# A four-block convolution kernel on one core: a new order of its units, a written-out TensorE program and a new head

## What is computed

```
x = x + attention(gn(x))      # block 0: windows of 4 x 4 pixels, 16 heads of size 1, softmax over 16 keys,
                              #          relative position bias, then a 16 x 16 projection
x = x + conv3x3(gn(x))        # block 1 ("conv1")
x = x + grid(gn(x))           # block 2: 16 cells, 4 columns x 4 rows; each a 3 x 3 convolution of up to 48
                              #          channels to "right", "up" and "down", with bias and relu;
                              #          the last cell's "right" is the output
x = x + quantised_conv(gn(x)) # block 3: x scaled by the largest value over all 8 images, rounded, 3 x 3
```

## Time and profile before

| | us |
|---|---|
| median of three runs | 3185.96 |
| lowest and highest | 3176.93, 3187.13 |
| the profiled execution | 3186.43 |
| its span, first to last instruction | 3184.6 |
| TensorE busy in the span | 2787.8 (88%) |
| VectorE busy | 2328.2 (73%) |
| ScalarE busy | 2012.8 (63%) |

### The profile page before, as it was taken

How to read it: one execution, slowest core, us unless ns; L and a number is a source line. 1 busy time by engine, 2 the same in 40 slices (tenths; PEclk the granted TensorE clock), 3 DMA queues, 4 the chain that set the end, 5 groups by cost and what they waited for, 6 DMA issues and landing times.

```text
span 3184.6 us, 86914 instructions
## 1 busy us (share of the span) xinstructions
PE 2787.8 (88%) x39155; PEld 1177.1 (37%) x39155; DVE 2328.2 (73%) x2062; ACT 2012.8 (63%) x2317; POOL 23.3 (1%) x68
## 2 busy tenths in 40 slices
PE   3564799989999899989999899989998998989976
PEld 2552233333333333333333333333333343333323
DVE  7978995889878895889688995899698971240135
ACT  1103976677767676767767676766766775766624
POOL 0000000000000000000000000000000000000000
PEclk9886899999999999999999999999999999999998
DMA  2003566577756866477756766587657755685667
GB/s 62 7 4 51 77 78 90 75 93 103 88 89 82 113 73 98 62 98 99 89 81 88 107 74 94 72 112 84 82 83 95 100 77 77 85 111 72 79 87 180
DMA packets 66136, 268.42 MB, mean 84 GB/s; under 512 B 48848, under 2 KB 49488, under 8 KB 53328
## 3 DMA queue, kind: packets, MB, share of 16 engines
q1 hardware_dynamic: 65744, 262.57, 60.2%
HBM read 22.54 MB, written 12.04 MB: 11 GB/s over the span
## 4 chain that ended last, share of the span: by engine, by line
PE 68%; DVE 13%; ACT 9%; issue 7%; SPq 1%; DMA 1%; POOLq 0%; POOL 0%; DVEq 0%; ACTq 0%
PE conv_banks L827 43%; PE conv_banks L841 19%; ACT pair L680 4%; ACT half L680 3%; DVE half L1030 2%; PE side_banks L788 2%; DVE score_max L1119 1%; DVE pair L1030 1%; PE stat_bank L798 1%; ACT scores L666 1%; PE side_banks L754 1%; PE conv_banks L926 1%; DVE pair L1116 1%; PE conv_banks L862 1%; DVE scores L1045 1%
## 5 line engine op out<-in xcount | busy, mean ns | idle before, releaser
L827 PE MATMUL conv_banks<-pair,w_cells 128*32 128x392 f32 x17664 | 1542.9, 498 | 48.2 <-issue 30.3
L680 ACT ACTIVATE pair<-conv_banks,b_cells 32x784 f32<-32x784 f32 x1316 | 1214.0, 923 | 568.4 <-PE conv_banks L841 502.4
L841 PE MATMUL conv_banks<-half,w_cells 64*32 64x392 f32 x18432 | 879.7, 509 | 140.0 <-ACT pair L680 60.1
L827 PEld LDWEIGHTS conv_banks<-pair,w_cells 128*32 128x32 f32 x17664 | 550.7, 109 | 983.3 <-issue 925.1
L680 ACT ACTIVATE half<-conv_banks,b_cells 32x392 f32<-32x392 f32 (+1 forms) x780 | 520.9, 668 | 199.9 <-PE conv_banks L841 128.0
L841 PEld LDWEIGHTS conv_banks<-half,w_cells 64*32 64x32 f32 x18432 | 339.5, 108 | 661.2 <-issue 611.6
L1030 DVE TENSOR_SCALAR half<-conv_banks,b_cells 32x392 f32<-32x392 f32 (+1 forms) x180 | 114.4, 636 | 327.1 <-PE conv_banks L841 168.8
L1030 DVE TENSOR_SCALAR pair<-conv_banks,b_cells 32x784 f32<-32x784 f32 x220 | 227.5, 1034 | 111.8 <-PE conv_banks L841 101.7
L1043 DVE TENSOR_TENSOR scores<-qkv 128x1792 f32<-128x1792 f32 x98 | 197.9, 2020 | 94.9 <-ACT qkv L661 94.7
L666 ACT ACTIVATE scores<-scores 128x1792 f32<-128x1792 f32 x104 | 176.7, 1699 | 101.1 <-DVE scores L1121 57.5
L1053 DVE TENSOR_REDUCE score_max<-scores 128x112 f32<-128x1792 f32 x98 | 197.9, 2020 | 9.5
(11 more groups left out here) (100 smaller groups left out, 1093.9 us busy)
## 6 DMA issues: line engine op xcount, KB each, us to landing
pair<-pair SPq DMA_DIRECT2D x384, 391.9 KB, 8.6
half<-half SPq DMA_DIRECT2D x352, 192.4 KB, 5.4
x_block<-in_x SPq DMA_DIRECT2D x64, 98.0 KB, 5.3
stream<-in_xs SPq DMA_DIRECT2D x8, 784.0 KB, 9.1
x_scratch<-stream SPq DMA_DIRECT2D x7, 784.0 KB, 7.7
pair<-x_scratch SPq DMA_DIRECT2D x7, 784.0 KB, 14.2
out_dram<-pair SPq DMA_DIRECT2D x4, 1120.0 KB, 5.4
half<-half SPq DMA_DIRECT2D x176, 7.1 KB, 4.6
```

Source lines behind the costliest of these rows:

```text
L680: done = nc.scalar.activation(dst, src, ACT.Relu, bias=b_ap)
L827: done = nc.tensor.matmul(conv_ps[32 * q:32 * q + 32, n + b, 0:QN], w, P[row][:, QG * s + BG * (q // 2):QG * s + BG * (q // 2 + 1), BX * ( ...
L841: done = nc.tensor.matmul(conv_ps[32 * q:32 * q + 32, n + h, 0:QN], w_all[rows, at:at + 32], T[rows, QG * u + BG * (q // 2):QG * u + BG * ...
```

## The change

- The list of units is one text (`ORDER`, a star marks the units of the later columns, which belong to the earlier image). It mixes units of different cells, where the list before went cell by cell; which cell a unit opens is found by `starts`.
- VectorE's share of the emptying is named unit by unit and by stop: `("s", j)` is behind scores j, `("w", j)` behind weigh j. In a middle round it has 18 units (before: the 20 of column 0), in round 6 43 (before 20), in round 7 10 (before 16), in round -1 one (before none). `finish` and the move of the stream have other stops.
- The side steps of TensorE, ScalarE and SP stand at other places, in all rounds.
- TensorE's loop over rounds 0 to 4 is written out; the other engines keep theirs.
- The head: x is laid out on the host so that it comes in one transfer; TensorE's first steps and VectorE's statistics wait only for what they read; ScalarE runs one small exponential at the start; the position bias is also laid out transposed (`first_rel`); the maximum over 16 keys is four `max` operations on halves; the last sums come in another order; the first stream is normed ahead of the next image's statistics; and the halos of the first image's normed input are issued half by SP and half by ScalarE.

The core of the diff (of the tables those of a middle round, and round -1's and the others' only in part):

```diff
-BODY = [((3, 0), 1), ((2, 2), 1), ((3, 1), 1), ((2, 3), 1), ((0, 0), 0), ((3, 2), 1), ((0, 1), 0), ((3, 3), 1),
-        ((0, 2), 0), ((1, 0), 0), ((0, 3), 0), ((1, 1), 0), ((1, 2), 0), ((2, 0), 0), ((1, 3), 0), ((2, 1), 0)]
-EARLY_BODY = [x for x in BODY if not x[1]]
-LATE_BODY = [x for x in BODY if x[1]]
...
+ORDER = """
+30D0* 30D1* 22D0* 22U0* 22D1* 22U1* 22R0* 00R0 22R1* 23U0* 23U1* 31D0* 31D1* 23R0* 23R1* 00D0 00D1
+00R1 32D0* 32D1* 01D0 01U0 01U1 01R0 01D1 33R0* 33R1* 10D0 10D1 01R1 02U0 02R0 02U1 02R1 02D0 10R0
+02D1 10R1 11U0 11D0 11U1 03U0 03U1 11D1 11R0 11R1 12U0 12U1 03R0 12D0 03R1 20D0 12D1 20D1 12R0 20R0
+20R1 12R1 21D0 21U0 21U1 21D1 21R0 13U0 13U1 13R0 13R1 21R1
+"""
+def unit(text):
+    return (int(text[0]), int(text[1])), "RUD".index(text[2]), int(text[3])
+def units(text):
+    return [unit(t) for t in text.split()]
+UNITS = units(ORDER)
+UNITS_F = [unit(t) for t in ORDER.split() if t[4:] != "*"]
+UNITS_L = [unit(t) for t in ORDER.split() if t[4:] == "*"]
...
-PE_MID = {2: [("qkv", 1, 0)], 7: [("proj", 0, 0), ("qkv", 2, 0)], 12: [("proj", 1, 0), ("qkv", 3, 0)],
-          27: [("proj", 2, 0), ("qkv", 4, 0)], 44: [("proj", 3, 0), ("qkv", 5, 0)],
-          49: [("proj", 4, 0), ("qkv", 6, 0)], 54: [("proj", 5, 0)], 59: [("proj", 6, 0)], 60: [("mean1", 0, 0)],
-          61: [("var1", 0, 0), ("mean0", 0, 1)], 62: [("var0", 0, 1)], 64: [("qkv", 0, 1)],
-          65: [("conv1", 0, 1)], 66: [("conv1", 1, 1)], 67: [("mean2", 0, 1), ("var2", 0, 1)]}
...
+            5: [("proj", 0, 0)], 8: [("qkv", 2, 0)], 13: [("proj", 1, 0), ("qkv", 3, 0)],
+            19: [("proj", 2, 0), ("qkv", 4, 0)], 25: [("proj", 3, 0), ("qkv", 5, 0)],
+            32: [("proj", 4, 0), ("qkv", 6, 0)], 41: [("proj", 5, 0)], 42: [("proj", 6, 0)],
+            43: [("mean1", 0, 0), ("var1", 0, 0), ("mean0", 0, 1), ("var0", 0, 1)], 45: [("qkv", 0, 1)],
+            46: [("conv1", 0, 1)], 47: [("conv1", 1, 1)], 49: [("mean2", 0, 1), ("var2", 0, 1)]}
+PE_MID = {1: [("qkv", 1, 0)], 8: [("proj", 0, 0), ("qkv", 2, 0)], 14: [("proj", 1, 0)], 17: [("qkv", 3, 0)],
+          29: [("proj", 2, 0)], 30: [("qkv", 4, 0)], 42: [("proj", 3, 0)], 43: [("qkv", 5, 0)],
+          48: [("proj", 4, 0)], 51: [("qkv", 6, 0)], 57: [("proj", 5, 0)], 60: [("proj", 6, 0)],
+          61: [("mean1", 0, 0), ("var1", 0, 0), ("mean0", 0, 1), ("var0", 0, 1)], 63: [("qkv", 0, 1)],
+          64: [("conv1", 0, 1)], 65: [("conv1", 1, 1)], 66: [("mean2", 0, 1)], 67: [("var2", 0, 1)]}
...
+ACT_MID = {1: [("qkv", 1, 0), ("exp", 1, 0)], 7: [("exp", 2, 0)], 8: [("qkv", 2, 0)], 10: [("exp", 3, 0)],
+           11: [("exp", 4, 0)], 17: [("qkv", 3, 0)], 19: [("exp", 5, 0)], 25: [("exp", 6, 0)],
+           34: [("qkv", 4, 0)], 37: [("exp", 7, 0)], 43: [("exp", 8, 0), ("qkv", 5, 0)], 45: [("exp", 9, 0)],
+           48: [("exp", 10, 0)], 51: [("qkv", 6, 0), ("exp", 11, 0)], 56: [("exp", 12, 0)],
+           57: [("exp", 13, 0)], 62: [("qkv", 0, 1)], 67: [("exp", 0, 1)]}
...
+SP_FIRST = {0: [("xb", 1)], 1: [("input", 0)], 29: [("xa", 2)], 42: [("conv1", 1)], 43: [("xb", 2)],
             49: [("input", 1)]}
-SP_MID = {35: [("x3", -1)], 48: [("xa", 2)], 63: [("conv1", 1)], 66: [("xb", 2)], 67: [("input", 1)]}
-SP_BEFORE = {35: [("x3", -1)], 62: [("conv1", 1)], 67: [("input", 1)]}
-SP_LATE = {35: [("x3", -1)]}
+SP_MID = {52: [("x3", -1), ("xa", 2)], 54: [("conv1", 1)], 67: [("xb", 2), ("input", 1)]}
...
-SHARED_FIRST, SHARED_MID, SHARED_LATE, SHARED_LAST = [], [(0, 0), (0, 1), (0, 2), (0, 3)], [(0, 0), (0, 1), (0, 2), (0, 3)], [(3, 0), (2, 2), (3, 1), (2, 3), (3, 2)]
...
+VEC_FIRST = {("w", 0): "00D1"}
+VEC_MID = {("w", 0): "22D0",
+           ("s", 5): "23R0 23R1 00D0 00D1",
+           ("s", 6): "01D0 01U0 01U1 01R0 01D1",
+           ("s", 7): "01R1 02U0 02R0 02U1 02R1 02D0 10R0 02D1"}
+FINISH_AT = ("s", 11)
+MOVE_AT_FIRST, MOVE_AT = ("s", 9), ("w", 13)
+VEC_LATE = """22U0 22U1 22R0 31D1 23R0 23R1 00D0 00D1 00R1 32D0 32D1 01D0 01U0 01U1 01R0 01D1 10D1 01R1 02U0 02R0
+02U1 02R1 02D0 10R0 02D1 11U1 03U0 03U1 11R0 12U0 12U1 03R0 12D0 03R1 20D0 12D1 20R0 12R1 21U0 21U1
+13U0 13U1 13R0"""
+VEC_LAST = """22U0 22R1 23U0 23U1 31D0 31D1 23R0 23R1 32D0 32D1"""
+SHARED_FIRST, SHARED_MID = [[u for text in at.values() for u in units(text)] for at in (VEC_FIRST, VEC_MID)]
+SHARED_LATE, SHARED_LAST = units(VEC_LATE), units(VEC_LAST)
...
+                sp.dma_start(XA[:], xa[i]).then_inc(x_in, 16)
...
+                if isinstance(i, int) and i == 0:
+                    send_side(sp, INPUT, 0)
+                    send_seam(sp, INPUT, 0)
+                else:
+                    send_half(sp, INPUT)
...
+            def first_halo(which):
+                act.wait_ge(c_ready, (which + 1) * NQ)
+                send_side(act, INPUT, 64)
+                send_seam(act, INPUT, 1)
...
+            act.wait_ge(half_set, 1)
+            nc.scalar.activation(warm[:], minus_half[:], ACT.Exp).then_inc(warmed, 1)
...
-            with pe.Fori(0, B - 3) as m:
+            for m in range(B):
                 body(m)
-            body(B - 3)
-            body(B - 2)
...
-                if k >= 1:
+                if 1 <= k < WROWS - 1:
                     first_num(k - 1)
...
+            first_num(WROWS - 2)
+            first_num(WROWS - 1)
             side_step(-2, "proj", WROWS - 2)
-            first_num(WROWS - 1)
             side_step(-2, "proj", WROWS - 1)
...
-                    rel = relb[:].rearrange("p (a b) -> p b a", b=WPX).unsqueeze(2).to_broadcast(shape)
+                    rel = first_rel.rearrange("p (b a) -> p b a", b=WPX).unsqueeze(2).to_broadcast(shape)
                     e4 = e.rearrange("p b (w a) -> p b w a", a=WPX)
                     first.inc(nc.vector.tensor_tensor(e4, q, key, ALU.mult))
                     first.wait()
                     first.inc(nc.vector.tensor_tensor(e4, e4, rel, ALU.add))
                     first.wait()
+                    first.inc(nc.vector.tensor_tensor(first_max, e[:, 0:8], e[:, 8:16], ALU.max))
+                    first.wait()
+                    for n in (4, 2):
+                        first.inc(nc.vector.tensor_tensor(first_max[:, 0:n], first_max[:, 0:n], first_max[:, n:2 * n],
+                                                          ALU.max))
+                        first.wait()
                     dve.wait_ge(scores_ready, j)
-                    first.inc(nc.vector.tensor_reduce(mx[:], e.rearrange("p b n -> p n b"), AX.X, ALU.max))
+                    first.inc(nc.vector.tensor_tensor(mx[:], first_max[:, 0], first_max[:, 1], ALU.max))
                     first.wait()
...
+                first_divide(WROWS - 1)
                 residual(0, WROWS - 2)
-                first_divide(WROWS - 1)
-                turn(0, first, None, True)
+                xb = XB[:].rearrange("p g w -> p (g w)")
+                dve.wait_ge(x1_ready, WROWS - 1)
+                for c in range(NQ - 1):
+                    first.inc(nc.vector.bn_stats(st1[:, c, :], xb[:, c * QN:(c + 1) * QN]))
+                residual(0, WROWS - 1)
+                dve.wait_ge(x1_ready, WROWS)
+                first.inc(nc.vector.bn_stats(st1[:, NQ - 1, :], xb[:, (NQ - 1) * QN:]))
+                first.hold()
+                nc.vector.bn_aggr(mv1[:], st1[:].rearrange("p c k -> p (c k)")
+                                  ).then_inc(norm_sems[1]["meanvar_ready"], 1)
+                norm(0, 1, first, mv1, dev1[:], nm1)
+                normalise_stream(1, nm1, 0)
+                dve.wait_ge(x_in, 2 * 16)
+                block_stats(0, XA[:], st0, mv0, first)
+                norm(1, 0, first, mv0, nm0[:, 3:4], nm0)
+                normalise_chunk(1, 0)
...
+            def other_work(m, at):
+                early = isinstance(m, int) and m < 0
+                empty(m, units((VEC_FIRST if early else VEC_MID).get(at, "")))
+                if at == FINISH_AT and not early:
+                    finish(m, m)
+                if at == (MOVE_AT_FIRST if early else MOVE_AT):
+                    move_stream(m + 1)
...
```

More of the change, by code:

```diff
@@ L153, in count_halos @@
             wrote(m, "input", INPUT)
-        for (cell, late) in body_of(m):
-            need[m, cell] = [(key, n[key]) for key in in_places(*cell)]
-            for o in cell_outs(*cell) if cell != LAST else []:
+        for k, (cell, o, u) in enumerate(units_in(m)):
+            if starts(m, k):
+                need[m, cell] = [(key, n[key]) for key in in_places(*cell)]
+            if u == 1 and cell != LAST:
                 wrote(m, (cell, o), out_place(*cell, o))
-        if m == -1:
-            n_first = dict(n)
     return need
@@ L179 @@
 PE_FIRST = {0: [("qkv", 0, 0), ("conv1", 0, 0), ("conv1", 1, 0), ("mean2", 0, 0), ("var2", 0, 0), ("qkv", 1, 0)],
[L180 to L184, removed]
@@ L191 @@
[L191 to L197, removed]
-             13: [("exp", 5, 0)], 16: [("exp", 6, 0)], 19: [("qkv", 4, 0), ("exp", 7, 0)], 23: [("exp", 8, 0)],
```

(44 more changed lines are left out.)

135 lines of the change are left out of this document (73 added, 62 removed).

## The result

The changed kernel takes 3141.2 us (median of 4 runs, 3134.7 to 3144.0) against 3186.6 for the kernel before in the same session: a ratio of 0.986, 95% interval 0.984 to 0.989. It is faster, but by 45 us where 172 were forecast, and 3141 lies above the range of 2980 to 3095. Its profiled execution (3140.0 us, 3138.3 in the span) is the one read here.

A forecast was written before the change was run, and what follows sets the result against it. TensorE was taken as the bound from 289.6 us on, VectorE's attention before. Round -1 ending at 523, + 5 x 333 + 331 + 310 + 115 + 68.1 of tail + 1.8 gave 3014 us; range 2980 to 3050, to 3095 with rival 1.

The forecast's parts named there:

- Head: Everything before the first unit: 41 us less (4 to 48), with the first unit's matmuls at 248 us.
- Scores and table load: In the head: faster bias addition and maximum save 26 us together; moving the table load ahead saves 1.3.
- The start: Start of the head: x in one transfer and earlier statistics, beginning near 9.8 us, gain 4 (3 to 5.5).
- The part between the last residual and the first unit: End of head: norming the stream first and sharing halo issuing between SP and ScalarE gain 3 us (2 to 5).
- Round -1: Round before round 0: moving ScalarE work to VectorE and four small units among large ones saves 8.5 us (0 to 15).
- TensorE's loop: Round edges: writing out the loop removes four jumps, 34 to 39 us; 14 if only the first gap were the jump's.
- New order and shares: Middle rounds: TensorE's 324.3 us floor plus 8.4 of waits, 333 a round (325 to 342).
- signs of being wrong: Rounds staying at 342 us, VectorE without a gap in them, or ScalarE standing at the edge.
- Rival 1: Rounds: the order gives nothing, VectorE comes late and each round keeps its 17 us: 3089 us; chance 0.26.
- Rival 2: Round edges: stalls move to ScalarE's loop, its jump costing 8 us; 24 us more, 3038; chance 0.10.
- Rival 3: Round edges: the stall isn't the loop's, written-out code changes nothing and 34 us stay: 3048; chance 0.05.
- Rival 4: SP's queue: 20R and 21U stand behind SP's wait, costing 29 us in each of six rounds: 3188; chance 0.03.

The follow-up runs named there:

- b_pe: The kernel before with only TensorE's loop over the rounds written out: 3162.6 us, ratio 0.993.
- a_peloop: The changed kernel with TensorE's loop put back as it was: 3207.2 us, ratio 1.007 to the kernel before.
- a_local: The changed kernel with halos cut to one group of rows only behind units at places 24 to 37 of rounds 0 to 6: 3097.2 us.
- a_act: The changed kernel with ScalarE's loop written out too: 3125.7 us, ratio 0.982 to the kernel before.
- a_light: The changed kernel with light halos: one group of rows per transfer, same number and signals, neighbours' borders wrong: 3007.5 us, ratio 0.945 to the kernel before.

## Why the prediction was wrong, step by step

**Head: right in sum, by two errors that cancel.** 41 forecast, 40.4 measured (289.64 to 249.26 for the first unit). Scores and table load came as costed. The start gave 8.4 us for 4: the statistics begin at 5.1, not 9.8 (the transfer is issued at 0.75, first of all, and lands within 4.4 us; the 9.1 us of the earlier trace rows are the median of eight loads of the stream, most of which go beside halos). The part between the last residual and the first unit takes 52 us and took 50; I had 3 less. The order of the norms and ScalarE's share of issuing together gained nothing there; no run takes them apart.

**Round -1: right.** The two together put its end at 524.4 for 523.

**TensorE's loop: the sign right, the term mis-sized.** 34 to 39 us forecast, 20 measured in the order from which it was read (b_pe). The price was then carried into another order, where it is 66 (a_peloop).

**New order and shares: the planning right, the cover wrong.** This step failed, at "TensorE's 324.3 us" as a floor and at a list of waits in which only semaphores stand. With light halos its rounds are 333.2, 331.8, 334.7, 334.6, 334.6, 330.2 and 304.5 against 333 five times, 331 and 310: 2304 in sum for 2306. TensorE's waits are 53 us there, 7.6 a round for the forecast 8.4. So order, shares and stops were costed rightly for a kernel whose instructions are on time, which this one is not: of its own signs of being wrong two came true, rounds above 342 and ScalarE standing at the edge, for which the sum had 1.4 us a round. Left out was that the instructions themselves arrive through the same DMA engines as the halos. The halos' bytes cost the new order 133 us in these rounds, 31 in the old one. Of the 133, 86 is standing and 47 is TensorE's busy time (2297.5 against 2250.5 over the seven rows). The lower clock explains the greater part of the 47 at most: the mean granted clock of the seven rounds is 0.982 against 0.994, a loss of 44 against 14 us even if TensorE was busy throughout. The rest wasn't taken apart. By place: the halos sent at places 24 to 37 account for 46 (a_local); ScalarE's written-out loop gives back 18 (rounds 0 to 6 of a_act take 2419). If these two add up, some 70 are spread over the other places; no run takes them apart. Why the new order is so much more exposed was only argued: the halos of 10D, 01R, 02U, 02R, 02D and 10R are sent within 30 us (2435.7 to 2465.6 in round 5), and the units that run meanwhile are small ones, at which TensorE starts 48 matmuls in 2.2 us and so uses up its instructions twice as fast as at a large one's 48 in 4.2.

**Rival 1**, "the order gives nothing", gave 3089 and comes nearer to the time, but its mechanism is refuted: TensorE's waits for VectorE come to 15 us in the seven rounds, where it had 17 a round left over. **Rival 2** is right that ScalarE's jump stalls, for 53 us in all; writing it out is worth 15 us, not its 24, since TensorE's own fetches are late behind the same transfers (57.0 us of its waits became 70.4). **Rival 3** is refuted by b_pe. **Rival 4** too: no wait for 20R or 21U appears. The trouble behind SP's queue was in the DMA engines, and it struck the instructions.

**Round 7** took 109.9 for 115 forecast; the wait before (3,2) is gone.

The Trainium skill (Runtime: NRT & Kernel Launch, Instruction fetch mechanics) says that crossing a page of instructions is mostly hidden. The traces disagree where the DMA engines are loaded: 39.4 and 17.6 us of TensorE's waits in straight code. It says too that a taken branch whose target lies outside the pages it holds must fetch it first, with which ScalarE's 9.7 us agree, and a_light's 0.35 shows how little that need cost. The Trainium skill (DMA: Bandwidth & Descriptors, Queues, rings and completion order) says that each DMA engine goes round its queues packet by packet, a packet being several descriptors. The packet of q8 that starts only within 0.1 us of 2475.4 agrees with a fetch that waits its turn. If shorter rows made shorter packets, a fetch should get through sooner: ScalarE's stalls agree (53.4 to 22.1 us), TensorE's don't (57.0 to 52.9).

## What to carry to other kernels

A plan made of engine times alone has a hidden term: instructions are DMA traffic. Where a profile shows "issue" inside a straight run of matmuls, look for the packet of instructions that lands just before the engine goes on and at what was sent in the 10 to 30 us before. Then test it by cutting the bytes while leaving every signal; that one run separated a good order from a crowded one. Don't take the price of a jump from one schedule into another. To spread the large transfers over the list as evenly as the engines' work is the next thing to try; no run here does it, and moving the stream's load alone changed nothing.

## What was not expected of the hardware

- Straight code of TensorE stood 3.00 and 4.05 us inside a unit for instructions, with DMA engines busy 65% of a round (0.65 in the rows); at 4% it did not stand there.
- Instructions came in packets of 16,384 bytes over the 16 DMA engines that also move the halos, and TensorE went on 1.2 to 1.9 us behind the end of a late one.
- ScalarE's jump cost 9.7 us or 0.35 by the halos' bytes alone. TensorE's four jumps cost 20 us in one order and 66 in another.
- Halo transfers in 448-byte packets instead of 24.5 KB (391.9 KB in 16 rows) carried the same bytes, all but 2%, with a landing only 1.2 to 1.5 us later and the DMA engines busy 75% of rounds 0 to 6 instead of 65%.
- After a stop of 6.5 us, 48 matmuls took 6.8 us instead of 4.2, at a granted clock of 0.60: a late instruction is paid more than once.
